# Latent attention: float16 halves of the probabilities turned by DMA, context scores beside the own ones, and a new order of mix, projection and scores on TensorE

## What is computed

```python
def layernorm(x, g, b):
    mu = jnp.mean(x, axis=-1, keepdims=True)
    var = jnp.mean(jnp.square(x - mu), axis=-1, keepdims=True)
    return (x - mu) * jax.lax.rsqrt(var + LN_EPS) * g + b

def rmsnorm(x, gamma):
    n = jnp.linalg.norm(x, axis=-1, keepdims=True) * x.shape[-1] ** (-0.5)
    return x / jnp.maximum(n, RMS_EPS) * gamma
```

## Time and profile before

| | us |
|---|---|
| median of 3 runs | 4354.94 (4354.06 to 4364.68) |
| the profiled execution | 4338.51, span 4336.5 |
| PE busy | 3656.8 (84%) |
| DVE busy | 3121.2 (72%) |
| ACT busy | 2715.1 (63%) |
| POOL busy | 1788.4 (41%) |
| latent attention, from its first norm transposes to its last addition | 3006.5 to 3759 |

### The profile page before, as it was taken

The page is one execution under the profiler, slowest core; times in us unless marked ns, Lnnn a source line. Parts: engine busy times, 40 slices in busy tenths (PEclk is TensorE's granted clock), DMA queues, the critical chain, the costliest instruction groups (busy, mean ns, idle before and its releaser), DMA issues. The chain is left out here.

```text
span 4336.5 us, 67381 instructions
## 1 busy us (share of the span) xinstructions
PE 3656.8 (84%) x22224; PEld 2915.7 (67%) x22224; DVE 3121.2 (72%) x6401; ACT 2715.1 (63%) x3957; POOL 1788.4 (41%) x994
## 2 busy tenths in 40 slices
PE   6877424257999999999999999995889898889999
PEld 4545311135777777777777777773777677779999
DVE  4567777875877887788877878883878687844347
ACT  3344347765877877787877878872657565543443
POOL 0044310005766767666766667751120202054005
PEclk9989756588999999999999999997889898879999
DMA  1057500006877878787877878881000000233224
GB/s 46 4 110 130 102 1 0 1 1 160 148 137 136 149 135 141 135 143 137 145 137 139 148 137 150 152 153 29 1 2 1 2 2 1 101 119 114 76 72 148
DMA packets 1272110, 395.01 MB, mean 91 GB/s; under 512 B 1208150, under 2 KB 1265623, under 8 KB 1270487
## 3 DMA queue, kind: packets, MB, share of 16 engines
q1 hardware_dynamic: 1265623, 373.89, 44.7%
q0 software_dynamic: 6144, 16.79, 1.2%
HBM read 49.00 MB, written 39.58 MB: 20 GB/s over the span
## 5 line engine op out<-in xcount | busy, mean ns | idle before, releaser
L2116 DVE TENSOR_REDUCE d_neg_max<-psum 128x1 f32<-128x1024 f32 x512 | 625.2, 1221 | 336.6 <-PE psum L1857 333.7
L2003 ACT ACTIVATE psum<-psum,d_bias 128x1024 f32<-128x1024 f32 x512 | 558.1, 1090 | 383.8 <-DVE d_bias L2120 383.1
L1857 PE MATMUL psum<-d_KH,d_QH 128*128 128x512 f32 x2048 | 683.2, 415 | 13.5 <-POOL d_KL L1824 7.8
L1857 PE MATMUL psum<-d_KL,d_QH 128*128 128x512 f32 x2048 | 638.5, 393 | 0.0
L1857 PE MATMUL psum<-d_KH,d_QL 128*128 128x512 f32 x2048 | 637.0, 392 | 0.0
L2125 DVE SCALAR_TENSOR_TENSOR d_halves<-psum,d_halves 128x1024 f16<-128x1024 f32 x512 | 622.6, 1216 | 14.9 <-ACT d_halves L2010 14.0
L2010 ACT ACTIVATE d_halves<-psum 128x1024 f16<-128x1024 f32 x512 | 520.6, 1017 | 3.2
L1857 PEld LDWEIGHTS psum<-d_KH,d_QH 128*128 128x128 f32 x2048 | 362.9, 189 | 140.8 <-issue 73.2
L1824 POOL TENSOR_TENSOR d_KL<-d_KC,d_KH 128x1024 fp32r<-128x1024 f32 x128 | 307.3, 2401 | 338.5 <-ACT d_KH L1999 338.5
L1857 PEld LDWEIGHTS psum<-d_KL,d_QH 128*128 128x128 f32 x2048 | 385.5, 188 | 86.5
L1857 PEld LDWEIGHTS psum<-d_KH,d_QL 128*128 128x128 f32 x2048 | 385.5, 188 | 86.4
(11 more groups left out here) (465 smaller groups left out, 8066.4 us busy)
## 6 DMA issues: line engine op xcount, KB each, us to landing
f_weights_raw<-in_L_ffn_packed_dram SPq DMA_DIRECT2D x10, 1088.0 KB, 15.5
f_tile<-expert_rows SPq DMA_DIRECT2D x71, 128.0 KB, 2.2
f_expert_out<-f_tile SPq DMA_DIRECT2D x71, 128.0 KB, 1.7
d_probsT<-d_halves SPq DMA_TRANSPOSE x512, 4.3
f_tile<-f_kept_rows SPq DMA_DIRECT2D x64, 128.0 KB, 2.1
expert_rows<-d_group_mixT SPq DMA_DIRECT2D x7, 1024.0 KB, 11.3
residual_stream<-in_x_dram SPq DMA_DIRECT2D x4, 1024.0 KB, 9.5
f_kept_rows<-residual_stream SPq DMA_DIRECT2D x4, 1024.0 KB, 8.6
```

Source lines behind the costliest of these rows:

```text
L1857: last = t.matmul(scores_at(u)[:, cols], q_part[:, ch, j * P:(j + 1) * P], k_part[hh % 2][:, ch, cols], start=k == 0, stop=k == 5)
L2003: a.activation(scores_at(u), scores_at(u), ACT.Exp, bias=bias[u % 2][:, 0:1])\
L2116: v.tensor_reduce(neg_max[u % 2][:], scores_at(u), AXIS.X, ALU.max, negate=True)\
```

## The change

It replaces nearly the whole stage; the other stages stay.

- The probabilities of a unit, own and context together (1102 columns with one pad), are one exponential into SBUF. ACT copies them to float16 (`high`), POOL subtracts to get the float16 low part (`low`), and SP's queue turns both halves, 2304 columns with padding, in one DMA transpose per unit. The transposes on PE and the copies and subtractions out of PSUM go.
- The context keys get a high and a low part in the preparation, and scores(u) has two matmuls of 78 columns more, beside the own scores. The separate phase of context scores goes; DVE adds the mask to the 78 columns in PSUM in each unit, and one maximum covers 1102 columns.
- Values are three bfloat16 parts instead of two float32r ones. The mix has 18 matmuls against the first two parts (128 columns of weights) and 18 against the third (64 columns of weights, the two halves of the probabilities to two halves of PSUM's partitions).
- The order in a PE step: an older pair's mix (odd steps from 5 on) or projection (even steps from 6 on) comes first, the scores of the unit second. On ACT a step is copy_mix (even steps from 6 on), exps, high.
- The batch loop is written out; the mixes and projections that are left over at the end of a batch, and its additions, are interleaved with the first steps of the next batch's first phase (14 steps, the values in steps 8 to 11). The next batch's norm is spread over DVE's and POOL's steps.

The diff, cut to its core:

```diff
+        probs = [over_work(f"probs{i}", [P, W], i * (WP - 32) * 4) for i in range(3)]
+        left = [sb(f"v_left{i}", [P, H, HD]) for i in range(2)]
+        halves = [sb(f"halves{i}", [P, 2, WP], F16) for i in range(3)]
+        probsT = [sb(f"probsT{i}", [P, 2 * KB, 2, P], F16) for i in range(2)]
...
+                for g in range(ALL):
+                    p, i = g // 2, g % 2
+                    if i == 0 and p >= 2:
+                        sp.wait_ge(mixed.sem, mixed.at(p - 1))
+                    sp.wait_ge(probs_low.sem, probs_low.at(g + 1))
+                    sp.dma_start_transpose(probsT[p % 2][:, :, i, :], halves[g % 3][:].rearrange("p a s -> p (a s)"))\
+                        .then_inc(turned[g % 4].sem, 16)
...
+                    if u >= 2:
+                        t.wait_ge(probs_ready.sem, probs_ready.at(g - 1))
+                    query = QS[:, h, j * P:(j + 1) * P]
+                    for half in range(2):
+                        cols = slice(half * HALF, (half + 1) * HALF)
+                        t.matmul(scores_at(u)[:, cols], query, KH[:, h, cols], start=True, stop=False)
+                        t.matmul(scores_at(u)[:, cols], query, KL[:, h, cols], start=False, stop=True)
+                    t.matmul(scores_at(u)[:, S:W], query, ctx_KH[:, b, h, :], start=True, stop=False)
+                    t.matmul(scores_at(u)[:, S:W], query, ctx_KL[:, b, h, :], start=False, stop=True)\
+                        .then_inc(scored.sem, 1)
...
+                def mix_values(b, p):
+                    h, pair = p % H, PAIRS * b + p
+                    if p == 0:
+                        t.wait_ge(v_low.sem, v_low.at(TB * (b + 1)))
+                    t.wait_ge(turned[2 * pair % 4].sem, unit_turned(2 * pair))
+                    t.wait_ge(turned[(2 * pair + 1) % 4].sem, unit_turned(2 * pair + 1))
+                    t.wait_ge(mixT_ready.sem, mixT_ready.at(pair))
+                    def moving(part, k):
+                        return probsT[pair % 2][:, part * KB + k, :, :].rearrange("p i q -> p (i q)")
...
+                            t.matmul(mix_bank, V[:, k, h, 0:2 * HD], moving(part, k), start=k + part == 0, stop=False)
...
+                    for part in range(2):
+                        t.matmul(mix_bank, ctx_values[:, b, h, 0:2 * HD], moving(part, TB)[0:Z, :], start=False,
+                                 stop=False)
+                    for k in range(TB):
+                        for part in range(2):
+                            t.matmul(mix_bank[part * HD:(part + 1) * HD, :], V[:, k, h, 2 * HD:3 * HD],
+                                     moving(part, k), start=False, stop=False)
+                    for part in range(2):
+                        last = t.matmul(mix_bank[part * HD:(part + 1) * HD, :], ctx_values[:, b, h, 2 * HD:3 * HD],
+                                        moving(part, TB)[0:Z, :], start=False, stop=True)
+                    last.then_inc(mixed.sem, 1)
...
+                def project(b, p):
+                    pair = PAIRS * b + p
+                    t.wait_ge(mixT_ready.sem, mixT_ready.at(pair + 1))
+                    t.wait_ge(added.sem, added.at(2 * pair))
+                    for i in range(2):
+                        last = t.matmul(out_at(i), mixT[pair % 2][:, i, :], wo[:, p % H, :], start=True, stop=True)
+                    last.then_inc(projected.sem, 1)
+                def behind(b, u):
+                    if u >= 5 and u % 2 and (u - 5) // 2 < PAIRS:
+                        mix_values(b, (u - 5) // 2)
+                    if u >= 6 and u % 2 == 0 and (u - 6) // 2 < PAIRS:
+                        project(b, (u - 6) // 2)
...
-                    for u in range(U + 4):
-                        if u < U:
-                            scores(u)
-                        if 0 <= u - 1 < U:
-                            turn(u - 1)
-                        if u % 2 == 0:
-                            if 0 <= u // 2 - 1 < PAIRS:
-                                turn_context(u // 2 - 1)
-                            if 0 <= u // 2 - 2 < PAIRS:
-                                project(u // 2 - 2)
-                        elif 0 <= (u - 3) // 2 < PAIRS:
-                            mix_values((u - 3) // 2)
...
+                    for u in range(U):
+                        behind(b, u)
+                        scores(b, u)
+                for s in range(STEPS):
+                    behind(B - 1, U + s)
...
+                def low(i):
+                    g.wait_ge(probs_high.sem, probs_high.at(i + 1))
+                    g.tensor_tensor(halves[i % 3][:, 1, 0:W], probs[i % 3][:], halves[i % 3][:, 0, 0:W], ALU.subtract)\
+                        .then_inc(probs_low.sem, 1)
...
-                    for u in range(U + 4):
-                        if u % 2 == 0 and 0 <= u // 2 - 2 < PAIRS:
-                            copy_mix(u // 2 - 2)
-                        if 0 <= u - 1 < U:
-                            high(u - 1)
-                        if u % 2 == 0 and 0 <= u // 2 - 1 < PAIRS:
-                            high_context(u // 2 - 1)
-                        if u < U:
-                            exps(u)
...
+                def copy_mix(pair):
+                    a.wait_ge(mixed.sem, mixed.at(pair + 1))
+                    a.wait_ge(projected.sem, projected.at(pair - 1))
+                    a.activation(mixT[pair % 2][:].rearrange("p i q -> p (i q)"), mix_bank, ACT.Copy)\
+                        .then_inc(mixT_ready.sem, 1)
+                def exps(g):
+                    p, i = g // 2, g % 2
+                    a.wait_ge(max_ready.sem, max_ready.at(g + 1))
+                    a.wait_ge(probs_low.sem, probs_low.at(g - 2))
+                    a.wait_ge(inverted.sem, inverted.at(p - 1))
+                    a.activation(probs[g % 3][:], scores_at(g), ACT.Exp, bias=neg_max[g % 2][:, 0:1],
+                                 accum_out=sums[p % 2][:, i:i + 1]).then_inc(probs_ready.sem, 1)
+                def high(g):
+                    a.wait_ge(probs_ready.sem, probs_ready.at(g + 1))
+                    if g >= 3:
+                        a.wait_ge(turned[(g - 3) % 4].sem, unit_turned(g - 3))
+                    a.activation(halves[g % 3][:, 0, 0:W], probs[g % 3][:], ACT.Copy).then_inc(probs_high.sem, 1)
+                def behind(b, u):
+                    if u >= 6 and u % 2 == 0 and (u - 6) // 2 < PAIRS:
+                        copy_mix(PAIRS * b + (u - 6) // 2)
...
+                    for u in range(U):
+                        behind(b, u)
+                        exps(U * b + u)
+                        high(U * b + u)
+                for s in range(STEPS):
+                    behind(B - 1, U + s)
...
+                def maximum(b, u):
+                    g = U * b + u
+                    v.wait_ge(scored.sem, scored.at(g + 1))
+                    v.tensor_tensor(scores_at(u)[:, S:W], scores_at(u)[:, S:W], lowered[:, b, :], ALU.add)\
+                        .then_inc(masked.sem, 1)
+                    v.wait_ge(masked.sem, masked.at(g + 1))
+                    v.tensor_reduce(own_neg_max[g % 2][:], scores_at(u), AXIS.X, ALU.max, negate=True)\
+                        .then_inc(own_max.sem, 1)
+                    v.wait_ge(own_max.sem, own_max.at(g + 1))
+                    v.wait_ge(probs_ready.sem, probs_ready.at(g - 1))
+                    v.tensor_scalar(neg_max[g % 2][:], own_neg_max[g % 2][:], LIFT, None, ALU.add)\
+                        .then_inc(max_ready.sem, 1)
```

More of the change, by code:

```diff
@@ L2480, in stage_latent_attention @@
-        raw = [over_turns(f"raw{i}", [P, G8, HD], i * ROW) for i in range(3)]
-        square = over_turns("square", [P, G8, HD], 3 * ROW)
-        unit = [over_turns(f"unit{i}", [P, G8, 2, HD], (4 + 2 * i) * ROW) for i in range(2)]
-        probs = [sb(f"probs{i}", [P, S + Z]) for i in range(2)]
-        pT_high, pT_low = ([over_turns(f"probsT_{k}{i}", [P, TB + 1, 2, P], (2 * i + (k == "low")) * TURN, F32R)
-                            for i in range(2)] for k in ("high", "low"))
+        ctx_act.passed(DC + 2 * B + 1)
@@ new lines, in turn_norm @@
+                def turn_norm(b, k):
+                    half, ch = k // 2, k % 2
+                    t.wait_ge(n.normed.sem, n.normed.at(TB * b + 4 * half + 4))
+                    t.wait_ge(probs_ready.sem, probs_ready.at(U * b - (1 if k < 3 else 0)))
+                    for q in range(4):
+                        last = t.transpose(bank(k)[:, q * P:(q + 1) * P], n.xn[:, 4 * half + q, ch * P:(ch + 1) * P],
+                                           core.ident[:])
+                    last.then_inc(n.turned.sem, 1)
@@ new lines, in turn_qk @@
+                def turn_qk(b, j):
+                    t.wait_ge(unit_ready.sem, unit_ready.at(TB * b + j + 1))
+                    t.wait_ge(probs_ready.sem, probs_ready.at(U * b))
+                    if j >= 2:
+                        t.wait_ge(qk_ready.sem, qk_ready.at(2 * (TB * b + j) - 2))
```

(33 more changed lines are left out.)

595 lines of the change are left out of this document (282 added, 313 removed).

## The result

The changed kernel takes 4650.3 us (median, 4647.6 to 4652.1) where the kernel before takes 4359.8 in the same comparison: ratio 1.0665, 95% interval 1.0645 to 1.0685, slower by 290 us. 4629 was forecast, with a range of 4480 to 4740. The profiled execution took 4651.06 us, span 4649.3.

The account below looks back on a forecast made before the run. PE and DVE in step were taken to bound the unit loop, PE waiting for DVE between batches. Loops +334, transitions -68 and +7.5 gave +274 on 4338.5, 4612, plus 16 for timed runs: 4629 us, range 4480 to 4740.

Parts of the forecast that it names:

- The new wait: Unit loop: PE's projection waits once per pair for ACT's copy of the mix, 4.96 us, bounds 4.6 and 5.4.
- PE's own work: Unit loop: projection, two units' scores and mix take PE 6.5 us per cycle at full clock.
- The clock: Unit loop: PE's clock drops after the idle in every cycle, costing 2.3 us, bounds 0 and 6.5.
- The cycle: Unit loop: one pair of units takes 13.8 us, 11.5 without the clock drop, against 7.36 before.
- Loop: Unit loop of a batch: 22 us, then thirteen cycles, 201.4 us against 117.8, +83.6; four times, +334.
- Between batches: From the end of scores(31) to the next batch's first scores: 55.3 us against 73.5, -18.2, three times.
- tail: End of the last batch: wait, three projections, two mixes, a late transpose, 16 us against 11.6, +4.5.
- The sum: Whole kernel: +334 for loops, -68 between batches and in the first, +7.5 for tail and preparation, +274 us.
- (a): Unit loop: same wait, but the clock holds, 120 us less than forecast, 4509 us; chance 0.22.
- (b): Unit loop: clock stays low all through, 6.5 instead of 2.3 us lost per cycle, 4847 us; chance 0.08.
- (c): Unit loop: the wait for the copy is hidden and DMA transposes pay, 4260 us; chance 0.04.
- (d): Whole kernel: change does less, short wait, clock held, transitions near 35 us, 4403 us; chance 0.02.

Follow-up runs that it names:

- third experiment: Changed kernel plus 36 idle PE matmuls of 256 columns ahead of each projection inside the unit loop, order and waits kept; ratio 1.0413 to the kernel before.
- the repaired kernels: Changed kernel with scores issued ahead of mix: everywhere (0.9851), also with copy ahead of exponential (0.9809), or odd steps only with copy and addition early (0.9804).
- the dose: Kernel with copy ahead of exponential and scores first, plus one further 256-column DMA transpose behind each transpose; ratio 0.9993 to the kernel before, against 0.9809 without.

## Why the prediction was right, step by step

- **The new wait**: 4.96 us was summed, 4.59 to 4.60 measured, 56 times as forecast. Eight shorter waits at the ends of batches (0.48 to 1.97 us) make up the 64 of the view. The lower bound of 4.6 was met because the hand-overs had been taken too long: lift 0.15 for 0.21, some 0.04 instead of 0.1 in front of `high`, ACT 0.04 after the lift's end for 0.18, PE 0.04 after the copy's end for 0.15. Mask 0.25 (0.24), maximum 1.30 (1.31) and `high` 1.12 (1.12) stood as summed.
- **PE's own work**: 6.5 us. With the clock held it is 6.4 (third experiment: a cycle of 11.17 less the 4.76 from the first filling matmul at 3151.98 to the projection at 3156.74). The two context matmuls took some 0.14 us together, not 0.26. The 18 half-width matmuls took 1.10 us, 1.12 was summed (third experiment, 3160.87 to 3161.97).
- **The clock**: 2.3 us per cycle was taken from the quantized stage, 2.5 measured, by the third experiment. This was the step with the least support, and the choice of the row with the nearest idle and work held. The Trainium skill ("TensorE: Matmul & The Clock Gate", section "HAM oscillation — how this bites in real kernels") says that a burst behind a wait starts at the lower level; here it does in every cycle, with projection and scores(e) at 1.2 GHz (granted clock 0.50 from 3197.57 to 3201.43). The prediction counted the quantized stage as agreeing, but there the trace agrees only with the low average: the burst right behind the 2.14 us was not slow (1.14 us), the groups after it were (1.89).
- **The cycle**: 13.8 for 12.6 at the start of a batch and 13.64 later. The first six steps took 22.1 us for 22. Loop: 201.4 predicted, 197.4 measured.
- **Between batches**: the mis-sized term. 55.3 us was predicted and 61.8 measured. Up to the first q and k it was as summed (10.9 for 10.3). Behind that, 50.9 instead of 45. The two late projections there wait 1.68 and 1.97 us for their copies, and the second is at the lower clock (2.02 us); one of the value steps waits 2.65 us for DVE and is slow too:

```profile
3277.79 2.02 PE L2630 MATMUL psum<-e_wo,e_mixT 128*128 128x256 f32 x4 [1.97 <-ACT e_mixT L2770]
...
3298.84 3.42 PE L2566 MATMUL psum<-e_wv,e_ln_xT 128*128 128x256 f32 x8 [2.65 <-DVE e_v_left L2844]
```

  "Short waits" had been given 5 us with two mixes and two projections in them; I had summed the waits at full clock.
- **What was there before** was off as well. Four loops of 117.8, the tail of 11.6 and the stage's end at 3759 leave 70.6 for a transition on average, not the 73.5 of the one that I looked at the earlier trace rows.
- **The sum**: the stage took 752.5 us before (3006.5 to 3759) and 1041.5 after (3002.9 to 4044.4), +289. Its parts: loops +318 (predicted +334), transitions 3 x (61.8 - 70.6) = -26 (-55), first batch -10 (-13), tail +7 (+4.5). Two errors of 16 and 29 us partly cancelled, which is luck. The profiled executions differ by 24 us more than the stage: 27 more behind it, in code that is the same in both (604.9 for 577.5 us, the two lengths named at the head of the experiments), and 4 less ahead of it, where the prediction had put +3. Between the medians the difference is 290.
- **The rivals.** (a), the clock holds: refuted; 2.07 us for the projection in each cycle where 1.13 is full clock. (b), low all through: refuted, the half-width matmuls take the 1.06 us of full clock in every cycle. (c), the wait hidden: its mechanism is what the repaired kernels do. 4260 was its price, 0.978 of the time before, and the best ones measured 0.980 and 0.981. But the point that I gave for it, whether ACT reaches the copy without having served scores(o), neither suffices nor is needed. Scores first alone reached 0.985 without it, and with it met in the changed kernel's order the ratio was 1.033. There the wait for `added` stood behind it, which I had not looked at, since it stands in the kernel before in the same form, and behind that the ring. (d), less than it says: refuted; the wait was at its low bound, but the clock fell and the transitions took 61.8 us, not 35.

What stays open: how much of the 1.01 us per pair in the dose is throughput and how much is per instruction; what a fourth buffer of `halves` gains; and whether the order with the mix first would lose nothing with the transposes a unit earlier, which would need a third buffer of `probsT` and wasn't tried.

## What to carry to other kernels

Lay the queues of all engines side by side over one period and ask of each wait what stands ahead of its releaser on the releaser's own engine: here a copy of 0.37 us cost 4.6 because an exponential and a conversion, both for work that PE had just issued, came first. Where an in-order engine has old work and new work in a slot, issue first what feeds the longest chain of other engines (here the scores) and let the old work, which nobody waits for soon, cover the way round. And take the waits behind the one that is late into the list: two more, never visible in the trace, stood between this kernel and its repair.

## What the runs showed of the hardware that I had not expected

- The length of the idle just before a projection doesn't alone decide its clock. After 0.63 us it took 1.13 us, and after 1.68 us, between batches, too. After 1.96 or 1.97 us it took 2.02 in the changed kernel, but 1.13 in two of three cases with the copy between exponential and `high`. After 2.86 us it took 2.04 in about two cycles of three and mostly some 1.6 in the third. After 3.44 us it took 2.07, except for the first of the loop in three of four batches (1.19 to 1.34), and after 4.59 us 2.07 always. The return to full clock came at different places for the same idle (cycles of 11.43 and 12.5 us with 3.44 us of idle each).
- Work that is thrown away can pay: 36 matmuls in place of a wait made the kernel faster by 0.025.
- A DMA transpose of 2304 float16 columns came every 3.4 us at a DMA share of 0.96, landed 4.7 us after issue in the median, and one more of 256 columns per unit cost 0.51 us and not the 0.38 of its columns.
